# Attention 2: the product with the values in two halves of 256 queries, one behind the second and one behind the fourth shifted product of a key block

## What is computed

```python
q = q.reshape(b, l, KVH, GROUPS, HD).transpose(0, 2, 3, 1, 4)
k = k.reshape(b, s, KVH, HD).transpose(0, 2, 1, 3)
v = v.reshape(b, s, KVH, HD).transpose(0, 2, 1, 3)
scores = jnp.einsum('bkgld,bksd->bkgls', q, k) * scale
scores = scores + encoder_attention_mask[:, :, None, :, :]
attn = jax.nn.softmax(scores, axis=-1)
out = jnp.einsum('bkgls,bksd->bkgld', attn, v)
```

## Time and profile before

| | us |
|---|---|
| median of 3 executions | 5834.13 (5833.36 to 5835.5) |
| the profiled execution | 5852.71 |
| its span, first to last instruction | 5850.9 |
| TensorE, VectorE, ScalarE, GpSimd busy | 5215.5, 3617.8, 2775.1, 1470.4 |
| mean granted clock of TensorE | 0.947 |

### The profile page before, as it was taken

How to read it: one execution, slowest core, us unless ns; L and a number is a source line. 1 busy time by engine, 2 the same in 40 slices (tenths; PEclk the granted TensorE clock), 3 DMA queues, 4 the chain that set the end, 5 groups by cost and what they waited for, 6 DMA issues and landing times. The chain is left out here.

```text
span 5850.9 us, 68584 instructions
## 1 busy us (share of the span) xinstructions
PE 5215.5 (89%) x25746; PEld 1833.2 (31%) x25746; DVE 3617.8 (62%) x4662; ACT 2775.1 (47%) x5277; POOL 1470.4 (25%) x708
## 2 busy tenths in 40 slices
PE   5987999999688899998688888886999999996999
PEld 2332433434233233332222222221433333322444
DVE  5548777878453777771588888882467777751110
ACT  2433333433222366663377777774236666662111
POOL 0004333434000366662000000000016666661000
PEclk9998999999799799999799999996999999998999
DMA  3233333333211323312111111111432323202000
GB/s 110 99 102 103 106 86 88 91 88 98 90 54 40 81 65 76 69 40 112 47 31 30 29 29 29 31 26 61 128 86 60 71 55 72 55 25 99 22 22 15
DMA packets 460340, 383.46 MB, mean 66 GB/s; under 512 B 170383, under 2 KB 359668, under 8 KB 459336
## 3 DMA queue, kind: packets, MB, share of 16 engines
q1 hardware_dynamic: 460000, 378.99, 24.0%
HBM read 242.83 MB, written 135.14 MB: 65 GB/s over the span
## 5 line engine op out<-in xcount | busy, mean ns | idle before, releaser
L2512 DVE TENSOR_REDUCE att_part<-att_scores 128x2 f32<-128x802 f32 x1024 | 964.9, 989 | 152.8 <-PE att_scores L2416 146.8
L2498 ACT ACTIVATE att_prob<-att_scores 128x512 f32<-128x512 f32 (+1 forms) x1664 | 861.4, 602 | 255.5 <-PE att_scores L2430 253.7
L3237 DVE TENSOR_REDUCE att_part<-att_scores 128x1 f32<-128x423 f32 x1280 | 677.3, 590 | 280.5 <-PE att_scores L2990 280.3
L3203 ACT ACTIVATE att_prob<-att_lower 128x512 f32<-128x512 f32 (+1 forms) x1088 | 562.7, 601 | 277.9 <-PE att_lower L3002 277.7
L1280 POOL TENSOR_TENSOR scan_z<-scan_r,scan_states 128x512 f32<-128x512 f32 x256 | 410.1, 1602 | 1073.3 <-DVE scan_states L1313 1060.5
L3223 POOL TENSOR_TENSOR att_acc<-att_acc,att_prob 128x1024 f32<-128x1024 f32 (+1 forms) x240 | 567.8, 2366 | 259.7 <-ACT att_prob L3203 258.5
L2205 DVE TENSOR_REDUCE att_part<-att_scores 128x1 f32<-128x401 f32 x1024 | 516.7, 567 | 186.8 <-PE att_scores L2042 185.6
L2430 PE MATMUL att_scores<-att_q,att_k 49*128 49x512 f16 (+1 forms) x1664 | 473.5, 392 | 109.2 <-ACT att_prob L2498 108.9
L2167 ACT ACTIVATE att_prob<-att_scores 128x512 f32<-128x512 f32 (+1 forms) x832 | 430.5, 600 | 238.1 <-PE att_scores L2054 237.9
L3223 POOL TENSOR_TENSOR att_acc<-att_prob 128x1024 f32<-128x1024 f32 x16 | 37.8, 2361 | 1739.1 <-ACT att_prob L3203 1739.1
L2416 PE MATMUL att_scores<-att_k,att_q 48*128 48x401 f16 x2048 | 428.8, 347 | 50.3 <-DVE att_part L2512 25.9
(11 more groups left out here) (322 smaller groups left out, 7248.0 us busy)
## 6 DMA issues: line engine op xcount, KB each, us to landing
v<-scan_val SPq DMA_DIRECT2D x96, 256.0 KB, 2.3
att_v<-v SPq DMA_DIRECT2D x32, 768.0 KB
att_spread<-recips SPq DMA_DIRECT2D x64, 256.0 KB
mix_plane<-in_mask SPq DMA_DIRECT2D x16, 800.5 KB, 6.7
att_k<-k1hi SPq DMA_DIRECT2D x32, 400.2 KB
att_k<-k3hi SPq DMA_DIRECT2D x32, 400.2 KB
scan_x<-in_ctx_t SPq DMA_DIRECT2D x12, 1024.0 KB, 8.4
o<-att_out SPq DMA_DIRECT2D x32, 256.0 KB, 2.0
```

What stands on the lines that cost most here:

```text
L2498: nc.scalar.activation(prob[g % NP][0:kw(kt), h, :], scores2[0:kw(kt), n % RING2, :], ACT.Exp).then_inc(exped, 1)
L2512: nc.vector.reduce_max(part[q % 2][:, :, ec, piece], scores1[:, bank["unit", p], :, 0:PIECE], AX.X).then_inc(reduced, 1)
L3203: nc.scalar.activation(prob[g % NP][0:kw(kt), h, :], scores2[0:kw(kt), n % RING2, :], ACT.Exp).then_inc(exped, 1)
L3237: nc.vector.reduce_max(part[q % 2][:, hc, piece:piece + 1], scores1[:, bank["piece", p], 0:PIECE], AX.X).then_inc(reduced, 1)
```

## The change

`mix` gets an argument `side`. For blocks 1 to 11 of a step side 0 multiplies the queries 0 to 255 and side 1 the queries 256 to 511; for blocks 0 and 12 side 0 does all 512 and side 1 nothing (these blocks start and end the sum in the bank). Side 0 stands behind the second shifted product and its unit, side 1 where the whole mix stood, behind the fourth. `mixdone` is raised once a block, with its last matmul.

```diff
-                def mix(s, kt):
+                def mix(s, kt, side):
                     g = s * NT + kt
+                    whole = kt in (0, NT - 1)
+                    if whole and side:
+                        return
+                    cols = slice(0, T) if whole else slice(side * T // 2, (side + 1) * T // 2)
                     if kt == 0:
                         pe.wait_ge(vloaded[s % 2], 16 * VLOADS * (s // 2 + 1))
                         if s:
                             pe.wait_ge(sumsout, s)
                     pe.wait_ge(exped, (g + 1) * QUAD)
                     for h in range(QUAD):
-                        ins = nc.tensor.matmul(sums[32 * h:32 * h + 32, :], V[s % 2][0:kw(kt), kt, :], prob[g % NP][0:kw(kt), h, :],
+                        ins = nc.tensor.matmul(sums[32 * h:32 * h + 32, cols], V[s % 2][0:kw(kt), kt, :], prob[g % NP][0:kw(kt), h, cols],
                                                start=kt == 0, stop=kt == NT - 1, tile_position=(0, 32 * h))
-                    ins.then_inc(mixdone, 1)
+                    if whole or side:
+                        ins.then_inc(mixdone, 1)
...
                             while issued < units_by(g, h):
                                 next(one)
                                 issued += 1
+                            if h == 1 and g >= LAG:
+                                mix(*divmod(g - LAG, NT), 0)
+                    elif g >= LAG:
+                        mix(*divmod(g - LAG, NT), 0)
                     if g >= LAG:
-                        mix(*divmod(g - LAG, NT))
+                        mix(*divmod(g - LAG, NT), 1)
```

## The result

| | median us | runs |
|---|---|---|
| before | 5833.74 | 5830.44 to 5835.5 |
| after | 5753.34 | 5752.69 to 5754.62 |

The ratio of the times is 0.9856, with a 95% interval of 0.9835 to 0.9876: 80.4 us less; the time lies in the predicted range, 4 us under the forecast. The profiled execution of after has a span of 5751.9 us.

What follows compares the result with a forecast made beforehand. Attention 2 was taken as bound by a ring of TensorE, VectorE and ScalarE, 2.62 us a block. Steps 63.6 plus end 13 save 76.6 from 5834.1, giving 5757.5 us; range 5715 to 5815.

Steps and rivals of the forecast that it cites:

- The ring before: Attention 2, ordinary block: shifted product, exp, fourth shifted product, unit and mix wait in a closed loop, 2.62 us a block.
- The price of a half: TensorE, mix of 256 columns: 0.57 us plus 0.10 to enter, 0.67; each split adds 0.24.
- Rival B: Short groups cost their weight load on top: blocks of 2.71 us, kernel slower at 5865; chance of slower 0.12.
- the 65-column row: Profile row of an fp32 matmul of 65 columns, 0.083 us over streaming each, evidence that short groups don't halve.
- the eight weight loads in 0.16: Timeline evidence that all loads of a mix fit in 0.16 us, under the 0.21 of one short group.
- The ordinary block: Attention 2 after the change: TensorE 2.27 us with three units, 2.10 with two, VectorE 2.23; taken as 2.28, 0.34 less.
- Blocks 1 to 3: Blocks around the drain of sums gain nothing: 8.1 to 8.2 us together, 8.0 before, with 3.10 from block 1 to 2.
- What is late next: VectorE's reciprocal and normalising product now show, 0.92 us; step 33.0, 2.05 less, 63.6 us over 31 steps.
- The end of the stage: Last 13 blocks of attention 2, without units: 19 us saved at full clock, 7 at half, 13 taken.
- A: Units waiting for reductions hold up TensorE's queue: ordinary blocks 2.45 us instead of 2.28, 5806; chance 0.13.
- C: Longer stall in the blocks round the drain makes the clock fall in every step: 25 us more, 5797; chance 0.06.
- D: Better than forecast: VectorE at its floor, 31.0 us a step, and the end at full clock, 5690; chance 0.03.

Runs made afterwards that it cites:

- 8: Kernel before the change, VectorE's reductions over 200 of each unit's 401 keys: 5789.7 us, steps of 34.24, one execution.
- 3: Changed kernel with the mixes still split but both halves behind the fourth shifted product: 5843.2 us, ratio 1.0016 to the kernel before.
- 6: Changed kernel with the split mixes in four quarters of 128 queries, one behind each shifted product: 6017.3 us, steps of 40.04.
- 7: Changed kernel with VectorE's reductions over 200 of each unit's 401 keys: 5681.5 us, steps of 30.79, one execution.
- Experiment 4: Changed kernel with the whole mixes of blocks 0 and 12 left behind the fourth shifted product: 5724.4 us, ratio 0.9794 to the kernel before.
- 1: Kernel before, unedited, profiled once more: 5832.8 us, last 13 blocks of attention 2 in 32.0 us.
- 9: Kernel before, unedited, profiled again: 5827.6 us, last 13 blocks of attention 2 in 32.0 us.
- 10: Changed kernel, unedited, profiled again on the same chip as the kernel before: 5753.3 us, steps 32.53, last 13 blocks 30.1 us.

## Why the prediction was right, point by point

*The ring before* (0.48+0.60+0.05+0.49+1.00 = 2.62, VectorE without a part) is shown by 8, where it stayed 2.62 with reductions at little over half their time.

*The price of a half* (0.57, and 0.10 to go in) measured 0.57 to 0.58 and 0.09 in the rows of after. Experiments 3 and 6 give its parts: streaming in proportion to the columns, 0.13 for every piece behind which TensorE goes back to the other form, nothing for a cut without that. Rival B is gone; the 65-column row was the wrong neighbour, the eight weight loads in 0.16 the right one.

*The ordinary block* (2.28) is 2.31 or 2.32. The two kinds have the same length for two reasons, as 7 shows: with three units it is TensorE (2.27 forecast, 2.31 measured; each of the two parts is 0.01 to 0.02 longer because the unit's matmuls start staggered on the two halves of the rows), with two it is VectorE (for TensorE alone 2.10 was forecast, and with the quick VectorE the block is 2.19; that staggering covers 0.04 of these 0.09 at most, the rest isn't traced). ScalarE was to be idle under 0.3 in a block, and the row of two such blocks shows 0.21.

*Blocks 1 to 3* (8.1 to 8.2) take 8.27, of which 3.10 between two third shifted products stand in the rows as forecast. Experiment 4 shows the same by taking it back: 0.70 a step.

*What is late next* is the step that was mis-sized. It added 0.92 for VectorE's reciprocal and normalising product, as if the whole of them came into the open, and left the block with the turn at 3.43. The step is 32.53, not 33.0. The normalising product shows as 0.16 (2.47 against 2.31 in its block), the reciprocal not at all, the block with the turn is 3.38: VectorE still had idle time to hide them, 92.1 us in the stage. Against this, the nine ordinary blocks, that 0.16 aside, came out 0.2 longer and blocks 1 to 3 0.1 longer than forecast. 31 undisturbed steps give 78 instead of 63.6.

*The end of the stage* (13 us) was wrong in its ground. Its two bounds, 19 and 7, both took the end of the one profiled execution, 44.8 us, as what the timed ones have. Experiments 1 and 9 show 32.0 there, and against that the end gives 1.9, and the last mixes 0.4. Even the full clock could have given only 4 to 5 from 32.0: by the prediction's own blocks the end is then 26.1+1.4 = 27.5, where 10, with short falls, has 30.1. The last block with a turn, ahead of that end, even got longer, 4.52 in 10 against 3.73 in 9: TensorE waits 1.58 there for the last maxima, where it waited 1.44, and a fall of the clock lies in it. The same mistake stands in the sentence that the 18.6 us between profile and median "should stay": they were this fall for the most part (12.8 in the last 13 blocks), and the profiled execution of after took 5753.7, within 0.4 of its median. What profile minus median was made of, the prediction didn't ask. The sizes of a block in the end were right: at 1.2 GHz 3.06 forecast and 3.10 in the rows, at 2.4 GHz 2.01 and 2.02.

So 63.6+13 = 76.6 came out beside 80.4 because 15 too little in the steps met 11 too much at the end. The mechanism is shown, and so is the size of a block; that the sum came so close is luck.

*The rivals.* A did not come: waits for reductions fell from 244.5 to 170.8. C did not come in the steps: both profiles after have four falls there, each of the three before six. It came in a small part at the end, with the short falls that before doesn't have. D's floor for VectorE was not reached.

## What to carry to other kernels

When a ring of few buffers runs through an in-order queue, what counts is the longest piece that stands between two links of it: cutting that piece helps only if the parts are put at different places of the ring (neither the cut nor the move alone gave anything), in even parts, and as few as do, since each entry has a fixed price, 0.23 us here (two were tried, and four). A piece that waits for something itself, as the mix behind the drain, is better left where its wait is over. And before a term is built on the end of a stage in one profile, look whether its clock is that of the timed executions: profile minus median was the hint.

## What the runs showed of the hardware

The fixed 0.23 belongs to going over from matmuls on half the rows (fp16) to matmuls on the four column groups (fp32) and back, not to the instruction: sixteen shorter matmuls in a row took the 1.00 of eight longer ones (3), and a quarter, a half and a whole mix hold TensorE 0.36, 0.57 and 1.00. Whether the tiles or the data type make the price, no run separates. The Trainium skill, "TensorEngine Tiling (Array Packing)", section Key Properties, says that a change of the tiling mode drains the engine. The runs fit that, with 0.23 us for both ways together.

The clock can fall in step with a loop. With all mixes behind the second shifted product it fell in every second step, each time in block 2 just as the drain began (0.14 to 0.28 us ahead of it), for 3.3 us of time lost; around such a fall TensorE stood idle in its wait for the drain:

```profile
3188.52 1.94 PE L2445 MATMUL att_sums<-att_prob,att_v 128*32 128x512 f32 x8 [0.53 <-issue]
```

With uneven pieces it fell in about every second step as well, also in block 2. With 32.53 a step and the same wait there were four falls in 31 steps. What makes the difference was not tried.
